# Decoder layer on one core: ScalarE writes the mask of slot 11, the mask matmul of that slot goes

## The reference

```
Q = split(query @ wq.T); K = split(key @ wk.T); V = split(value @ wv.T)     # 16 heads of 16
scores = einsum('bhqd,bhkd->bhqk', Q, K) / sqrt(16)
scores = where(mask[:, None] == 1, -1e9, scores)                            # mask: 112 x 375, one for all heads
attn = softmax(scores); out = attn @ V; out = out @ w_out.T
```

## Time and profile before

| | us |
|---|---|
| median of 3 timed runs | 1336.21 |
| lowest and highest of them | 1335.66, 1337.94 |
| the profiled execution | 1324.22 |
| its span (first to last instruction) | 1322.4 |
| TensorE busy in the span | 1221.1 |
| ScalarE busy in the span | 761.3 |

### The profile page before, as it was taken

How to read it: one execution, slowest core, us unless ns; L and a number is a source line. 1 busy time by engine, 2 the same in 40 slices (tenths; PEclk the granted TensorE clock), 3 DMA queues, 4 the chain that set the end, 5 groups by cost and what they waited for, 6 DMA issues and landing times.

```text
span 1322.4 us, 34415 instructions
## 1 busy us (share of the span) xinstructions
PE 1221.1 (92%) x10866; PEld 1107.4 (84%) x10866; DVE 899.4 (68%) x2932; ACT 761.3 (58%) x1780; POOL 498.6 (38%) x709
## 2 busy tenths in 40 slices
PE   5899999999997788999999999999999988999984
PEld 4788889899897677889999999899998777888884
DVE  4684664856746456788788888888887575555548
ACT  3444344333442226788888888888888854555530
POOL 2332240422412323344444444444444541333335
PEclk9999999999998898999999999999999898999997
DMA  8499700000000235566666665556665143333358
GB/s 206 106 232 239 176 0 0 0 0 0 0 0 23 57 76 140 141 142 153 153 149 154 152 151 148 145 147 150 152 157 148 52 136 93 101 106 98 106 141 249
DMA packets 131263, 151.39 MB, mean 114 GB/s; under 512 B 41107, under 2 KB 111108, under 8 KB 131156
## 3 DMA queue, kind: packets, MB, share of 16 engines
q1 hardware_dynamic: 124436, 134.55, 42.1%
q0 software_dynamic: 6160, 15.69, 3.5%
q10 hardware_dynamic: 576, 0.07, 0.0%
HBM read 79.27 MB, written 45.82 MB: 95 GB/s over the span
## 4 chain that ended last, share of the span: by engine, by line
PE 50%; DVE 4%; issue 2%; ACT 2%; DMA 2%; POOL 1%; SPq 1%; DVEq 0%; POOLq 0%; ACTq 0%
PE psum L875 9%; PE psum L1124 7%; PE psum L1161 6%; PE psum L1147 6%; PE psum L1296 6%; PE psum L1316 3%; PE psum L1093 2%; PE psum L1142 2%; PE psum L1189 2%; PE psum L1175 1%; DVE x_res L2333 1%; PE psum L1208 1%; PE psum L1287 1%; PE psum L1304 1%; DVE x_res L2327 1%
## 5 line engine op out<-in xcount | busy, mean ns | idle before, releaser
L2196 DVE CUSTOM_DVE_ANT_0 junk<-psum,biasq 112x375 f32<-112x375 f32 x512 | 267.5, 542 | 93.2 <-issue 60.1
L1653 ACT ACTIVATE pr<-psum 125x448 f32<-125x448 f32 x384 | 204.1, 540 | 37.5 <-PE psum L1147 35.8
L1147 PE MATMUL psum<-qst,kst 97*125 97x224 f32 x768 | 194.4, 319 | 5.4 <-ACT psum L1662 5.2
L1124 PE MATMUL psum<-kst,qst 96*112 96x376 f32 x512 | 170.1, 357 | 3.6 <-DVE smax L2196 3.2
L1147 PEld LDWEIGHTS psum<-qst,kst 97*125 97x125 f32 x768 | 139.2, 192 | 19.6 <-ACT psum L1662 13.2
L1662 ACT ACTIVATE psum<-flagk 125x448 f32<-125x448 bf16 x256 | 140.4, 549 | 6.7
L717 POOL TENSOR_TENSOR rs<-rs,neg_half 112x1 f32<-112x1 f32 x32 | 18.2, 569 | 244.3 <-DVE rs L2109 244.3
L841 POOL DMA_INDIRECT routed_y<-yb,yrow x61 | 58.7, 962 | 123.9 <-ACT yb L1843 119.7
L1124 PEld LDWEIGHTS psum<-kst,qst 96*112 96x112 f32 x512 | 89.8, 180 | 15.0 <-issue 5.8
L1161 PE MATMUL psum<-pr,vaug 125*32 125x112 f32 x3072 | 96.3, 267 | 0.0
L759 POOL DMA_INDIRECT routed_h<-h,slot x64 | 74.7, 1166 | 32.3 <-POOL h L748 14.8
(11 more groups left out here) (320 smaller groups left out, 3529.5 us busy)
## 6 DMA issues: line engine op xcount, KB each, us to landing
kst<-khi SPq DMA_DIRECT2D x64, 376.0 KB, 4.9
routed_h<-in_route_pad SPq DMA_DIRECT2D x6, 3640.0 KB
kst<-klo SPq DMA_DIRECT2D x32, 376.0 KB, 6.1
ctxT<-in_ctxT SPq DMA_DIRECT2D x32, 375.0 KB, 3.5
hblk<-routed_h SPq DMA_DIRECT2D x61, 130.0 KB, 2.1
qst<-qhi SPq DMA_DIRECT2D x128, 56.0 KB, 2.5
stage<-in_e SPq DMA_DIRECT2D x21, 256.0 KB, 3.1
maskq<-in_mask SPq DMA_DIRECT2D x32, 164.1 KB
```

The source lines that it names most:

```text
L1124: pe.matmul(bank[max_bank(n, par, hd)][0:T, 0:S2E], head(qst[par][0:ROWS], hd), pair(kst[par][0:ROWS], hd // 2), start=True, stop=True).th ...
L1147: mm = pe.matmul(bank[q % 2][0:KP, cols(i, 2 * T)], pair(kst[par], n)[:, cols(q // HPB, KP)], both(qst[par], n), start=False, stop=True, s ...
L1653: nc.scalar.activation(pr[q % PROBS][:].rearrange("k i q -> k (i q)"), bank[q % 2][0:KP, 0:GT], ACT.Exp, scale=1.0 / HD ** 0.5).then_inc(s ...
L2196: nc.vector.tensor_tensor_reduce(out=junk[:, hd % 2, :], in0=bank[max_bank(n, par, hd)][0:T, 0:S2], in1=biasq[:, par, :], scale=1.0, scala ...
```

## The change

ScalarE writes the mask of slot 11 too, right behind the exponentials of slot 9. TensorE's mask matmul of slot 11 goes, and the first score matmul of slot 11 waits for ScalarE's write in its place. Each sample then has 9 writes and 3 mask matmuls where it had 8 and 4. The condition in ScalarE's stream was q < 8 and becomes q != 8, so that the write of slot 10 stays where it was and the one of slot 11 is issued at q = 9.

```
-WRITTEN = (2, 3, 4, 6, 7, 8, 9, 10)
+WRITTEN = (2, 3, 4, 6, 7, 8, 9, 10, 11)
...
                     exponentials(t, par, q)
                     if q == 5 and following >= 2:
                         copy_h(*far)
-                    if q + 2 in WRITTEN and q < 8:
+                    if q + 2 in WRITTEN and q != 8:
                         write_mask(t, par, q + 2)
```

## The result

The changed kernel takes 1338.63 us in the median of 22 runs, the kernel before 1336.32 in 22 runs beside them: a ratio of 1.0019 with a 95% interval of 1.0012 to 1.0027, so 2.5 us more (1.6 to 3.6). The forecast was 1.2 us more, inside the range and within what I had called no measurable change. The direction was right and the size half of what came. One of the later timed runs (e_hoist_cover, 3903.8 us where its eleven others took 1321 to 1329) is left out of that kernel's ratio.

A forecast was written before the change was run, and what follows sets the result against it. TensorE was taken to bound the kernel. 28 samples x 0.03 = 0.8 us plus 0.35 for sample 30 made +1.2 on 1336.21, so 1337.4 us; range 1333.2 to 1340.0, with chance 0.72 of no measurable change (within 0.2%).

The forecast's parts named there:

- What bounds the kernel: Middle of the cross-attention: TensorE sets the pace, busy 49.78 of 50 us; slot 11's mask matmul is 0.19 us of its chain.
- its removal: Mask matmul of slot 11 gone from TensorE: 32 x 0.19 = 6.1 us would go if nothing took its place.
- given back: Rival: slot 11's weight load does not wait in full, up to 0.19 us gained per sample, 1330.1 us; chance 0.12.
- The added write: ScalarE, slot 9: write starts 0.58 us after the exponentials' start, lasts 0.55, covered by 0.71 us idle before slot 10's exponentials.
- The added wait: TensorE, slot 11: scores end 1.66 us after slot 9's exponentials start, as in slot 8; path 0.03 us longer than the matmul.
- What is behind the waiting load: TensorE after slot 11's wait: scores, row maxima, transposes and the next sample's slot 0 all come 0.03 us later.
- a dear hand-over in slot 11: Rival: slot 11's scores end 0.21 us later than before, 6.3 us on top, 1342.5 us; chance 0.16.
- The ends: Samples 0, 1 and 31 cost nothing; sample 30 costs 0.35 us, its slot 11 scores ending up to 0.39 us later.
- The sum: Whole kernel: 28 samples x 0.03 = 0.8 us, sample 30 0.35, others 0; together +1.2 us.
- The signs to look for: Profile after: 96 mask matmuls for 128, 288 writes for 256, ScalarE's wait before slot 10's exponentials from 0.71 to about 0.15 us.
- A doubling of the waits for L1662: Sign: TensorE's slot 11 load waits for that line in nearly every sample; about 55 waits, new ones about 0.2 us.
- A sample still takes 17.2 us: Sign: time per sample unchanged at 17.2 us; a move of 0.1 us would make the prediction wrong.

The follow-up runs named there:

- e_hoist_cover: Changed kernel with TensorE's four waits moved ahead of slot 11's wait and two transposes moved between scores of slots 10 and 11; periods 17.14 to 17.17 us, interval from 0.9995.
- e_free: Kernel before with slot 11's mask left out altogether, neither matmul nor write; 1.7 us faster by the timed ratio.
- e_dummy: Kernel before plus a spare ScalarE copy in the new write's place, for which nobody waits; periods 17.21 to 17.23 us, the ratio's interval holds 1.
- e_hoist: Changed kernel with TensorE's four waits for the next sample's first row-maximum matmul moved in front of slot 11's wait for the write; ratio 1.0029.
- the quiet profile: Second profile of the changed kernel, rerun without edit and free of the common stalls; span 1325.1 us, ratio 1.0032.
- e_cover: Changed kernel with the two transposes that opened the next sample moved between the scores of slots 10 and 11; ratio 1.0011.

## Why the prediction came out as it did

**What bounds the kernel.** Right: TensorE's chain goes through slot 11, and the period moves with it. But the matmul's 0.19 us was not all path. e_free gives 0.07 to 0.10 us a sample and 1.7 us in time (0 to 3.3) against the 6.1 that I had put down for its removal. I had the price of a matmul where the next wait behind it (the masks of slots 0 and 1 on the exponentials of slots 10 and 11) was 0.1 us away. That wait was in my own rows, the load at 815.80 just behind exponentials that end at 815.73; I used it only in the direction of a delay. So the rival "given back" was priced at two to four times its worth: 32 x 0.10 = 3.2 us by the periods, 1.7 by the clock.

**The added write.** Right in place and price: 0.58 us behind the exponentials, 0.55 long, covered; e_dummy shows the cover without the wait.

**The added wait.** Right: 1.66 us from the exponentials to the end of the scores, in slot 11 as in slot 8. That the load would be done when the write ends, on which the rival "given back" stood, no run shows. In both profiles of the changed kernel the first load of slot 11 starts 0.05 us behind the end of the write in all 32 samples, and in no run with the write before its end; so here no load came ahead of the write that it waits for.

**What is behind the waiting load.** This is the step that failed, though the time came out inside the range. I counted the array's instructions behind the wait and gave them all 0.03 us. What stands there too are the sequencer's waits for the next sample's first matmul, done ahead of time before and now only after the write. They add 0.17 to 0.2 us in 16 of 27 samples. The forecast 28 x 0.03 = 0.8 us was measured as 3.0 us over 27 of these samples, and e_hoist, with nothing moved but those waits, brings the undisturbed periods down to 17.24 to 17.27, which is the kernel before and the forecast 0.03. That the time stayed in the range is partly luck: its upper end came from a dear hand-over in slot 11, which was not there (the scores end 1.66 us behind the exponentials), and made room for a loss that no rival had.

**The ends.** Sample 1: the next one came as before (20.61 and 20.60 us), covered as forecast. Sample 30: 16.76 against 16.42 us in the second profile, so 0.34 where 0.35 was forecast. That is the period from the exponentials of slot 9 in sample 30 to those in sample 31; the one in front of it is 13.36 against 13.34. In sample 31 the exponentials of slot 11 end 2.51 us behind the start of those of slot 9, against 2.50: zero, as forecast.

**The sum.** 0.8 + 0.35 = 1.2 forecast, 3.0 + 0.34 by the quiet profile, 2.5 and 4.2 by the clock.

**The signs to look for.** The counts were right, and so was the fall of ScalarE's wait at slot 10, to 0.12 us. A doubling of the waits for L1662 was not seen: the view lists 35 in the first profile of the changed kernel and 28 in the second where it had 27. In front of the new ones the loads stand idle for 0.15 us, not 0.20, and the view puts most of them in one row with the loads of slot 10. "A sample still takes 17.2 us" was wrong in two of three samples of the loop; they moved by 0.2 us, and a move of 0.1 us was the sign by which the account was to be called wrong.

## What to carry to other kernels

A semaphore wait on TensorE can cost more than the time until its release: here the sequencer also stopped doing ahead of time the register arithmetic and the waits that stand behind it in the program, and they came out afterwards one by one (0.17 to 0.2 us for four of them). When a change makes an engine wait, count the sequencer's instructions up to the next matmul, and move those that are satisfied anyway in front of the new wait. Move only those: in samples 3 and 28 of e_hoist, and in samples 1 and 30 of e_cover, what was moved ahead was itself not ready and held everything up. And before work is taken off the busiest engine, look for the next wait behind it: if that is 0.1 us away, 0.1 us is what the work is worth.

## What the runs showed of the hardware that was not expected

Four waits with their register arithmetic, each recorded at 32 to 51 ns, come 0.1 us apart on TensorE's sequencer, in the kernel before (796.9 to 797.2) as in the changed one (801.5 to 801.8). They cost nothing while it is ahead of the array: in the kernel before, the load of L1124 behind them starts 1.36 us behind the exponentials of slot 9 out of sample 16, with four records, as out of sample 17, with two. Once it is behind they cost 0.17 to 0.2 us: in the second profile of the changed kernel that load starts at 1.57 us (to 1.65) where all four are recorded, and at 1.39 or 1.40 where two are, save out of sample 28.

In some groups of runs, ScalarE and VectorE stand still together, mostly for 1.1 to 1.6 us and mostly in the first sample of a turn of ScalarE's loop (VectorE's own program has no loop there), in every profiled kernel of the group and in none of the others. Between the two profiles of the changed kernel this is 481.4 - 469.4 = 12 us over the 27 periods, and the groups' times, 1334 to 1338 against 1322 us, differ by about as much. The first profile of the kernel before has none either, though the timed runs beside it took 1336 us. I haven't found what the two engines wait for.
